# Routing of a mixture-of-experts layer: counts for two tiles at once, another order of work for the first expert, fewer identity products, kept input tiles

## The reference, cut to what matters

```python
c = einsum('bct,bcd->bdt', x, w[conditions])        # y: one 128x128 matrix per block
probs = softmax(y @ gate_w.T)                       # 64 experts
w, sel = top_k(probs, 8); w = w / sum(w)
pos = cumsum(one_hot(sel))                          # slot of each token in its expert, 256 slots
out = (silu(inp @ wg) * (inp @ wu)) @ wd            # per expert, inp = its up to 256 tokens
x = x + sum over the experts of out * w
```

## Time and profile before

| what | us |
|---|---|
| median of 3 runs (2400.47 to 2400.88) | 2400.86 |
| the profiled execution | 2414.42 |
| its span, first to last instruction | 2412.7 |
| PE busy (matmul) | 2371.8 (98%) |
| DVE busy | 1739.5 (72%) |
| ACT busy | 1374.4 (57%) |
| POOL busy | 1408.7 (58%) |
| first identity product | 164.0 |
| first transpose of expert 0's rows | 180.1 |
| first product of expert 0, of expert 1 | 183.9, 218.1 |

### The profile page before, as it was taken

How to read it: one execution, slowest core, us unless ns; L and a number is a source line. 1 busy time by engine, 2 the same in 40 slices (tenths; PEclk the granted TensorE clock), 3 DMA queues, 4 the chain that set the end, 5 groups by cost and what they waited for, 6 DMA issues and landing times.

```text
span 2412.7 us, 35618 instructions
## 1 busy us (share of the span) xinstructions
PE 2371.8 (98%) x12877; PEld 2089.1 (87%) x12877; DVE 1739.5 (72%) x2905; ACT 1374.4 (57%) x2288; POOL 1408.7 (58%) x1032
## 2 busy tenths in 40 slices
PE   6998999999999999999999999999999999999999
PEld 4677888888888888888888888888879999999999
DVE  4877888888888887888888888887862255555554
ACT  4766777777677776777777777777751111111110
POOL 4107887777777777777777777777710032222221
PEclk9999999999999999999999999999999999999999
DMA  8988998989999899998989989899875254444441
GB/s 295 366 293 286 292 282 282 279 276 292 286 289 282 277 285 284 280 285 274 283 282 284 281 278 280 278 289 279 276 205 110 76 148 129 129 129 129 129 120 56
DMA packets 249457, 582.35 MB, mean 241 GB/s; under 512 B 82745, under 2 KB 106682, under 8 KB 249154
## 3 DMA queue, kind: packets, MB, share of 16 engines
q1 hardware_dynamic: 182306, 401.18, 50.8%
q0 software_dynamic: 55584, 160.02, 25.6%
q10 hardware_dynamic: 11392, 18.88, 2.1%
HBM read 460.71 MB, written 123.45 MB: 242 GB/s over the span
## 4 chain that ended last, share of the span: by engine, by line
PE 89%; ACT 1%; DVE 1%; DMA 1%; issue 1%; SPq 0%; ACTq 0%; DVEq 0%
PE ps L762 25%; PE ps L775 21%; PE ps L869 16%; PE ps L761 12%; PE ps L827 5%; PE ps L758 4%; PE ps L862 2%; PE ps L759 2%; PE ps L842 1%; PE ps L725 1%; ACT HR L1020 0%; DMA raw<-in_L_ffn_wd 0%; DMA bmR<-accd 0%; DVE LR L1435 0%; DMA x<-in_L_ffn_base_w 0%
## 5 line engine op out<-in xcount | busy, mean ns | idle before, releaser
L762 PE MATMUL ps<-XX,HR 128*128 128x512 f32 x2688 | 958.6, 396 | 0.0
L761 PE MATMUL ps<-XX,LR 128*128 128x256 f32 x2688 | 750.4, 279 | 0.0
L546 POOL DMA_INDIRECT Xg<-yd,idx x504 | 648.0, 1286 | 166.2 <-issue 152.6
L1435 DVE TENSOR_TENSOR LR<-raw,HR 128x1536 fp32r<-128x1536 f32 x384 | 657.3, 1752 | 5.7 <-issue 3.7
L762 PEld LDWEIGHTS ps<-XX,HR 128*128 128x128 f32 x2688 | 505.3, 188 | 103.7
L1020 ACT ACTIVATE HR<-raw 128x1536 fp32r<-128x1536 f32 x384 | 556.4, 1478 | 16.5 <-DMA raw<-in_L_ffn_wd 11.5
L761 PEld LDWEIGHTS ps<-XX,LR 128*128 128x128 f32 x2688 | 507.0, 189 | 17.7 <-issue 0.2
L568 POOL DMA_INDIRECT accd<-ot,toki x128 | 254.2, 1986 | 157.4 <-ACT ot L1074 136.0
L869 PE MATMUL ps<-MH,xT 128*128 128x392 f32 x1536 | 337.2, 345 | 0.0
L775 PE MATMUL ps<-HR,hH 128*128 128x512 f32 x768 | 300.0, 391 | 4.8 <-DVE hL L1479 4.8
L775 PE MATMUL ps<-LR,hH 128*128 128x512 f32 x768 | 303.6, 395 | 0.0
(11 more groups left out here) (203 smaller groups left out, 3344.0 us busy)
## 6 DMA issues: line engine op xcount, KB each, us to landing
raw<-in_L_ffn_wd SPq DMA_DIRECT2D x128, 768.0 KB
raw<-in_L_ffn_wg SPq DMA_DIRECT2D x126, 768.0 KB
raw<-in_L_ffn_wu SPq DMA_DIRECT2D x126, 768.0 KB
xt<-in_x SPq DMA_DIRECT2D x32, 512.0 KB
yd<-yrow ACTq DMA_DIRECT2D x32, 512.0 KB, 6.7
x<-accd SPq DMA_DIRECT2D x32, 512.0 KB, 5.0
out<-osb SPq DMA_DIRECT2D x31, 512.0 KB, 2.9
accd<-xt SPq DMA_DIRECT2D x24, 512.0 KB
```

Source lines behind the costliest of these rows:

```text
L546: eng.indirect_dma_start(Xg[:, c, q, :], None, yd4, bass.IndirectOffsetOnAxis(ap=idx4[:, e % 4, i:i + 1], axis=0))\
L761: eng.matmul(bank(out, 0, CAP), wl, xx[:, 0:CAP], start=False, stop=False)
L762: mm = eng.matmul(bank(out), wh, xx, start=False, stop=(k == 7))
L1435: eng.tensor_tensor(LR[:, (n + 2) % NHL, :], raw[:, n % NRAW, :], HR[:, (n + 2) % NHL, :].bitcast(F32), ALU.subtract).then_inc(s_L, 1)
```

## The change

- `counts`, `copy_c`, `store_c` and `tiles` take a pair of tiles: the same three products with 128 columns of mask or sum in place of 64, two ACT copies a pair, two stores of 64 rows issued together, two DVE sums of 128 columns a pair; `table_rows` adds the two halves of `tacc` at its end.
- The eight x tiles with i % 4 = 3 are kept in SBUF (seven in new buffers laid over later `HR` and `LR` buffers 0, 6 and 7), and SP stores them from there to `acc`: four after weight unit 1, four after unit 5. The DRAM-to-DRAM `fill` is gone. Units 0 to 3 wait for the stores of tiles 25 to 28, not 28 to 31. New waits: ACT's split of unit 4 for the first four stores, DVE's split of unit 4, ACT's of unit 6 and DVE's first `turn_x` for the last four; `direct_token(0)` for all stores of `yd`; scatter waits for the kept stores in place of the fills.
- `keep_busy`: 4, 10, 44 becomes 0, 8, 20.
- Expert 0's order on ACT and DVE is written anew: the weight splits, `share`, `turn_x`, `count`, `index(2)` and the splits of expert 1 change their places.

The diff, cut to its core:

```diff
@@ -118,10 +118,15 @@
-        sb("ygap0", [P, UN], F32, yts)
+        sb("ygap0", [P, 432], F32, yts)
+        xkA = sb("xkA", [P, 1, D], F32, yts)
+        sb("ygap1", [P, 80], F32, yts)
-        sb("ygap1", [P, (NHL - 1) * UN - 4096], F32, yts)
+        sb("ygap2", [P, 6 * UN - UN - 4096], F32, yts)
+        xkB = sb("xkB", [P, 3, D], F32, yts)
+        sb("ygap3", [P, 6 * UN - 4096], F32, yts)
+        xkC = sb("xkC", [P, 3, D], F32, yts)
@@ -181,6 +187,12 @@
         pre.close()
+        def xin(i):
+            n = i // 4
+            if i % 4 < NS or n == NB // 4 - 1:
+                return xt[:, i % 4, :]
+            return (xkB, xkC, xkA)[n // 3][:, n % 3, :]
+
         ar, lb, arp = x1[:, 4, :], x1[:, 5, :], x1[:, 1, :]
@@ -360,27 +372,25 @@
                     eng.dma_start(acc[j * P:(j + 1) * P, :], xt[:, j % 4, :]).then_inc(d_as[j % 4], 16)
-            rest = [i for i in range(NB) if i % 4 >= NS]
-
-            def fill(n):
-                i = rest[n]
-                if n >= 2:
-                    eng.wait_ge(d_ad[n % 2], 16 * (n // 2))
-                eng.dma_start(acc[i * P:(i + 1) * P, :], x_r[i * P:(i + 1) * P, :]).then_inc(d_ad[n % 2], 16)
+            def store_kept(n):
+                i = 4 * n + NS
+                eng.wait_ge(d_x[NS], 16 * (n + 1))
+                eng.dma_start(acc[i * P:(i + 1) * P, :], xin(i)).then_inc(d_ak[n // KEEP], 16)
...
                 if n < NRAW:
-                    i = NB - NRAW + n
+                    i = NB - NRAW - 3 + n
                     eng.wait_ge(d_ys[i % NY], 16 * (i // NY + 1))
...
                 load_unit(n)
-                if n == 7:
-                    for k in range(FILL):
-                        fill(k)
-                if n >= 8 and n - 8 + FILL < len(rest):
-                    fill(n - 8 + FILL)
+                if n == 1:
+                    for k in range(KEEP):
+                        store_kept(k)
+                if n == NRAW + 1:
+                    for k in range(KEEP, NB // 4):
+                        store_kept(k)
                 if n >= 100 and n % 4 == 0 and n < 100 + 4 * NA:
@@ -670,16 +680,18 @@
-            def counts(i):
-                eng.wait_ge(s_mask, 2 * i + 2)
-                if i >= 2:
-                    eng.wait_ge(s_cte, i - 1)
-                b = 6 + i % 2
-                eng.matmul(bank(b, 0, P, E), mask[:, i % 4, :], tri[:, :], start=True, stop=(i == 0))
-                if i:
-                    eng.matmul(bank(b, 0, P, E), macc[:, i, :], ones[:, :], start=False, stop=True)
-                eng.matmul(bank(b, P, P + E), ones[:, :], macc[:, i + 1, :], start=True, stop=True)\
-                   .then_inc(s_cum, 1)
+            def counts(q):
+                i = 2 * q
+                eng.wait_ge(s_mask, 2 * i + 4)
+                if q >= 2:
+                    eng.wait_ge(s_cte, q - 1)
+                b = 6 + q % 2
+                eng.matmul(bank(b, 0, P), mask[:, i % 4:i % 4 + 2, :].rearrange("p c e -> p (c e)"), tri[:, :],
+                           start=True, stop=False)
+                eng.matmul(bank(b, 0, P), macc[:, i:i + 2, :].rearrange("p c e -> p (c e)"), ones[:, :],
+                           start=False, stop=True)
+                eng.matmul(bank(b, P, 2 * P), ones[:, :], macc[:, i + 1:i + 3, :].rearrange("p c e -> p (c e)"),
+                           start=True, stop=True).then_inc(s_cum, 1)
@@ -716,8 +728,8 @@
                     direct_counts()
-                if i >= 6:
-                    counts(i - 6)
+                if i >= 7 and i % 2 == 1:
+                    counts((i - 7) // 2)
@@ -726,12 +738,11 @@
                 eng.wait_ge(s_yr, NB)
-                keep_busy(4)
                 direct_rows()
-                keep_busy(10)
+                keep_busy(8)
                 eng.wait_ge(s_tok, 2)
-                keep_busy(44)
-                eng.wait_ge(s_cte, NB)
+                keep_busy(20)
+                eng.wait_ge(s_cte, NB // 2)
                 for c in range(2):
@@ -963,18 +974,18 @@
-            def copy_c(i):
-                eng.wait_ge(s_cum, i + 1)
-                if i >= 4:
-                    eng.wait_ge(d_ts[i % 4], 16 * (i // 4))
-                if i >= 8:
-                    eng.wait_ge(s_cb, i - 7)
-                eng.activation(ct[:, i % 4, :], bank(6 + i % 2, 0, P, E), ACT.Copy)
-                eng.activation(cb[:, i % 8, :], bank(6 + i % 2, P, P + E), ACT.Copy).then_inc(s_cte, 1)
-
-            def store_c(i):
-                eng.wait_ge(s_cte, i + 1)
-                eng.dma_start(tab_v[i], ct[:, i % 4, :]).then_inc(d_ts[i % 4], 16)
+            def copy_c(q):
+                eng.wait_ge(s_cum, q + 1)
+                if q >= 4:
+                    eng.wait_ge(d_ts[q % 4], 32 * (q // 4))
+                    eng.wait_ge(s_cb, q - 3)
+                eng.activation(ct[:, q % 4, :], bank(6 + q % 2, 0, P), ACT.Copy)
+                eng.activation(cb[:, q % 4, :], bank(6 + q % 2, P, 2 * P), ACT.Copy).then_inc(s_cte, 1)
+
+            def store_c(q):
+                eng.wait_ge(s_cte, q + 1)
+                for c in range(2):
+                    eng.dma_start(tab_v[2 * q + c], ct[c * E:(c + 1) * E, q % 4, :]).then_inc(d_ts[q % 4], 16)
@@ -1003,10 +1014,10 @@
                     exps(i - 6)
-                if 7 <= i < NB + 7:
-                    copy_c(i - 7)
-                if 8 <= i < NB + 8:
-                    store_c(i - 8)
+                if 8 <= i < NB + 8 and i % 2 == 0:
+                    copy_c((i - 8) // 2)
+                if 9 <= i < NB + 8 and i % 2 == 1:
+                    store_c((i - 9) // 2)
                 if 7 <= i < NB + 3:
@@ -1015,6 +1026,10 @@
                 eng.wait_ge(d_raw[n % NRAW], 16 * (n // NRAW + 8))
+                if n == NRAW:
+                    eng.wait_ge(d_ak[0], 16 * KEEP)
+                if n == 6:
+                    eng.wait_ge(d_ak[1], 16 * KEEP)
                 if n >= NHL:
@@ -1088,21 +1103,36 @@
             split("uA", 0)
+            split("uB", 0)
+            eng.activation(sil[:, 0:1], pf[:, 0:1], ACT.Silu)
             for n in range(4):
                 high_0(n)
-            split("uB", 0)
+            split("dA", 0)
+            split("dB", 0)
+            copy_2(0)
+            silu(0)
+            high_h(0)
             for i in range(NB - 4, NB):
...
             store_w(NB - 1)
-            eng.activation(sil[:, 0:1], pf[:, 0:1], ACT.Silu)
-            split("dA", 0)
-            for e in range(E):
-                if 1 <= e < E - 2:
+            split("gA", 1)
+            copy_2(1)
+            silu(1)
+            high_x(1, 0)
+            high_h(1)
+            high_x(1, 1)
+            copy_2(2)
+            silu(2)
+            spread(2)
+            high_h(2)
+            for k in ("uA", "gB", "uB", "dA"):
+                split(k, 1)
+            for e in range(1, E):
+                if e < E - 2:
                     spread(e + 2)
-                if e >= 1:
-                    for o in range(4):
-                        result(e - 1, o // 2, o % 2)
-                if 1 <= e < E - 1:
+                for o in range(4):
+                    result(e - 1, o // 2, o % 2)
+                if e < E - 1:
                     high_x(e + 1, 0)
@@ -1310,7 +1335,7 @@
                 if i >= 4:
-                    eng.wait_ge(s_cum, i - 3)
+                    eng.wait_ge(s_cum, i // 2 - 1)
                 eng.tensor_scalar(mask[:, b, :], zr[:, b, :], MARK, None, ALU.is_ge).then_inc(s_mask, 1)
@@ -1346,8 +1370,8 @@
                     shift(a)
-                if i >= 8:
-                    tiles(i - 8)
+                if i >= 9 and i % 2 == 1:
+                    tiles((i - 9) // 2)
                 if a >= 1:
@@ -1401,6 +1424,9 @@
             def direct_token(e):
+                if e == 0:
+                    for s in range(NY):
+                        eng.wait_ge(d_ys[s], 16 * (NB // NY))
                 eng.wait_ge(s_g0, e + 1)
@@ -1503,19 +1532,46 @@
             index(1)
+            split("uA", 0)
             for n in range(4):
                 low_0(n)
-            split("uA", 0)
             split("uB", 0)
-            for i in range(NB - 3, NB):
-                tiles(i)
+            tiles(NB // 2 - 2)
+            tiles(NB // 2 - 1)
             table_rows()
-            for i in range(NB - 4, NB):
+            split("dA", 0)
+            join(0)
+            for i in range(NB - 4, NB - 2):
                 weigh(i)
                 invert(i)
-            split("dA", 0)
-            for e in range(E):
-                if 1 <= e < E - 1:
+            product(0)
+            for i in range(NB - 2, NB):
+                weigh(i)
+                invert(i)
+            low_h(0)
+            split("dB", 0)
+            join(1)
+            turn_x(1, 0)
+            product(1)
+            turn_x(1, 1)
+            low_h(1)
+            count(2)
+            token(2)
+            join(2)
+            low_x(1, 0)
```

(13 more changed lines are left out.)

82 lines of the change are left out of this document (31 added, 51 removed).

## The result

The kernel is slower. Median 2406.12 us (2403.45 to 2409.57, 16 runs) against 2401.55 (2399.91 to 2402.98, 16 runs) for the kernel before on the same chip: ratio 1.002, 95% interval 1.0014 to 1.0027, that is +4.6 us. I had predicted 2395.2 and faster. Measured again beside later runs it was 1.0026 (1.0017 to 1.0035).

A forecast was written before the change was run, and what follows sets the result against it. PE was taken to bound the kernel from expert 2 on, so only that rhythm's start could move: -8.5 at the transposes, -1.5 in expert 0, +4.3 back to POOL, -5.7 us, 2400.86 to 2395.2; range 2389.5 to 2399.5.

The forecast's parts named there:

- Counts in pairs: Routing loop: a pair of tiles costs PE 0.30 us for 0.54, saving 0.24 on 13 pairs, -3.1 us.
- 0, if the DMA engines are the bound after all: Routing loop: one bound of the -3.1 us for counts in pairs, no gain if DMA sets the pace.
- that rival: The routing loop is bound by DMA, so the counts give nothing: 2399.0 us, chance 0.17.
- Before the tokens and the gather: End of routing: first token step 4.6 us earlier, gather landed at 171.6, first transpose 8.5 us earlier.
- Over 9 us: Expert 0's gather: taking over 9 us was a named sign of being wrong; 6.6 was measured before.
- two splits and the load end at 171.2, under the cover of ACT's 8.25 us wait: ACT before expert 0: unit 3 lands by 167, so the early uB split and table load cost nothing.
- From transpose to first product 3.8 us stay: Start of expert 0: the distance stays 3.8 us, so expert 0 starts at 175.4.
- Expert 0, (b): `down` of expert 0: shorter waits for `hL` and gB, so expert 1 starts near 208 for 218.14, -10 us.
- (c): POOL's gathers for expert 2: start about 205 for 207.39, only -2.5 us; expert 3's rows come 5.7 earlier.
- The rival "slower": Expert 0: the last four kept stores land late and hold DVE; slower by over 0.2%, chance 0.05.
- The clock falls: Expert 0's first blocks: fewer identity products and a late gather let the clock halve; 2397.3 us, chance 0.09.
- The sum: Whole kernel: -8.5 at the transposes, -1.5 in expert 0, +4.3 given back to POOL, together -5.7 us.

The follow-up runs named there:

- e14: The changed kernel with no edit, measured and profiled again: 2407.25 us, ratio 1.0026 to the kernel before.
- e3: Changed kernel with ACT's split of uB and its table load put back behind `high_0`: 2405.48 us, ratio 1.0019 to the kernel before.
- e6: Changed kernel with DVE's `count(3)` and `token(3)` ahead of all five splits of expert 1: 2406.93 us, ratio 1.0026 to the kernel before.
- e10: Kernel before plus pairs, fewer identity products and expert 0's new order, no kept tiles: 2415.36 us, ratio 1.0003, in a slow-start series.
- e16: Changed kernel with only `count(2)`, `token(2)`, `spread(2)` and `index(2)` moved forward: 2401.37 us, ratio 1.0 to the kernel before.
- e9: Changed kernel with expert 0's old order on ACT and DVE, kept tiles staying: 2406.89 us, ratio 0.9971, in a slow-start series.
- e15: Changed kernel with the whole chain to expert 2's gathers forward (`index(2)`, `store_w`, `count(3)` ahead of the splits): 2400.85 us, ratio 0.9997 to the kernel before.
- e1: Kernel before plus counts in pairs alone, with the wait for y's stores: 2399.32 us, ratio 0.999 to the kernel before.
- e8: Kernel before plus counts in pairs and fewer identity products (0, 8, 20): 2394.55 us, ratio 0.9974 to the kernel before.
- e18: Changed kernel with the chain to expert 2's gathers forward and the split of uB behind `high_0`: 2398.54 us, ratio 0.9992 to the kernel before.

## Why the prediction was wrong

- **Counts in pairs**: right. Predicted -3.1 by 0.24 a pair; the rows say 0.33 a pair, but the last product with `wall` moved by -3.0 (-2.0 in e14), and the run alone gives -2.4 (interval -0.2 to -4.6). The third product costs nothing: I had put 0.30 for a pair, it is 0.18. The bound "0, if the DMA engines are the bound after all" and that rival fall with it.
- **Before the tokens and the gather**: right for the first transpose in this profile, with some luck. G moved by -4.0 for -4.6, the transposes by -8.35 for -8.5; in e14 it was -2.2 and -6.5. The second half of the gather was later than I said: it landed for 160.82, 9.7 us after G, with 2.23 us of waiting in the middle of the transposes. Over 9 us was one of the signs of being wrong that I had named.
- **"two splits and the load end at 171.2, under the cover of ACT's 8.25 us wait"**: wrong by 10.5 us. In the clock of the second profile that is 157; ACT ended them at 167.48. I had unit 3 landed by 167, 153 in that clock. In fact SP issued its last piece at 157.66. The step counted bytes (5.4 us at 385 GB/s) and not SP's own issue time, 13.01 and 11.56 us for 16 pieces each, with 3.3 us for the kept stores between; the earlier trace rows had the 9.90 us. So "From transpose to first product 3.8 us stay" failed: it was 13.0 us, and expert 0 started at 170.54 for 161.2.
- **Expert 0, (b)**: I said expert 1 would start 10 us earlier. It was 5.5, of which 4.0 had been won up to G. From expert 0's first product to expert 1's it took 27.5 us for 33.9 before, but only since it began so late; in e3, where it began after 1.57 us, it took 32.6. The last kept stores, which I had landed near 185 (171 in the second profile's clock), held DVE's split of dA until 177.08.
- **(c) "What is late next. POOL ... That chain gives about 205: only -2.5"** is the step that failed. I named the right chain, and took its start as 190.7 in the second profile's clock. It was 194.78, 4 us more, since `index(2)`, now behind the third block of expert 0 and not the second, slipped with everything ahead of it. It wasn't the first stop: in e3 expert 0 began 5.4 us earlier and the issue came at 195.30, because `join(0)` stood behind the wait for the kept stores. Then the first issue took 7.22 us in place of 0.94, of which nothing in the rows of before could warn me (e6 and e10 show that this part cost little); then the rows had to share the DMA engines with the weight units that the same four splits had set free. Together the second issue was 7.9 us later than before, not 2.5 earlier. With `index(2)` alone put forward (e16) S falls from 41.2 to 37.3 and the kernel is 6 us faster than the changed one beside it. I had turned the four splits over for what they do to DVE and never asked who stands still beside them and what they trigger.
- **The rival "slower"** had a part of the mechanism. The last kept stores did hold DVE, 2.90 us (5.27 in e14, 8.78 in e3), but e9 and e15, which wait for them too, have a small D. "The clock falls" did happen, 5 us at half clock behind each 8 us stop; it too was a sign that I had named. But it isn't bound to such long stops: 0.50 met expert 0 also in e3 and e1, behind stops of 1.57 and 1.90 us, and not in e8 or e18, behind 1.57. No run here separates what it cost.
- The profile I read was of a slow start; I took the 13.6 us between it and the median for something that lies around every profile. That changed no term of the sum, but it is a step that I didn't examine.

The sum, done again with what was measured: -4.0 up to G, then +9.1 (-2.2 and +7.0 in e14). The chain forward returns D to about 98, `keep_busy` is worth -2.9 of D where nothing else stops PE.

## What to carry to other kernels

When an order is rewritten, follow the work that starts a transfer for two steps later (index, gather, transpose) before the work of the step itself. That chain has no idle engine to show in the old profile, and moving it back by one block cost some 6 us here, more than either stop that the new order was meant to remove. The largest stop in a profile is worth what is left of it at the next meeting point: taking away 7 of 8.63 us brought nothing. What the runs suggest, without one that shows it alone: let gathers go well ahead of work that frees many buffers. One microsecond ahead (e6) brought next to nothing; with half of them out before it (e16) the gain came. And before a ratio is carried to another series, put one kernel in both.

## What the runs showed of the hardware

An indirect DMA issue of POOL, 0.94 us by itself, that began 0.36 us after DVE had begun fp32 subtractions of two tiles in SBUF without a gap, ended 0.82 us after the last of them, beside four (7.21 or 7.22 us in six profiles) as beside two (3.88 us). It isn't always so: in e10 it began 0.37 us after the first of four and took 2.21 us; POOL had been idle for 2.16 us ahead of it, for 3.64 to 6.11 in the others. And issues that directly followed another went on beside the splits, in e6 one for each split (2.25, 1.37, 1.36, 1.37 us, the last three begun 1.67 us apart, a split's own period), in e10 likewise. The Trainium skill (SBUF — State Buffer, Who interferes with whom) says that a DVE instruction with two SBUF inputs contends with a GpSimd instruction that reads SBUF, and calls the port pair that they share an exclusive lock. The one issue for each split agrees. Why the first one mostly stays out over three borders between splits, and in e10 didn't, no run here shows.

That the start of the routing loop can take 12 us more, in one execution by chance and in two series in all kernels, I had not expected either; no run here shows its cause.
